# Attention pooling: the fourth group's relu on ScalarE and the softmax steps in one run

## What is computed

```python
h = relu(einsum('bse,eh->bsh', behavior, W_b) + (candidate @ W_c)[:, None, :] + fc1_b)
scores = einsum('bsh,h->bs', h, fc2_w[:, 0]) + fc2_b[0]
attn = softmax(scores, axis=-1)
user_interest = einsum('bse,bs->be', behavior, attn)
z = relu(concatenate([user_interest, candidate], axis=1) @ mlp1_w + mlp1_b)
logit = (z @ mlp2_w + mlp2_b)[:, 0]
```

## Time and profile before

| what | value |
|---|---|
| median of 3 runs | 304.12 us (303.32 to 304.25) |
| the profiled execution's own time | 302.84 us |
| its span, first to last instruction | 301.0 us |
| PE busy | 274.9 us, 91% |
| DVE busy | 255.3 us, 85% |
| ACT busy | 109.7 us, 36% |
| POOL busy | 28.7 us, 10% |
| granted TensorE clock, mean | 0.989 |
| bytes moved by DMA | 105.83 MB |

### The profile page before, as it was taken

The page is one execution under the profiler, slowest core; times in us unless marked ns, Lnnn a source line. Parts: engine busy times, 40 slices in busy tenths (PEclk is TensorE's granted clock), DMA queues, the critical chain, the costliest instruction groups (busy, mean ns, idle before and its releaser), DMA issues.

```text
span 301.0 us, 8104 instructions
## 1 busy us (share of the span) xinstructions
PE 274.9 (91%) x2934; PEld 187.8 (62%) x2934; DVE 255.3 (85%) x437; ACT 109.7 (36%) x267; POOL 28.7 (10%) x38
## 2 busy tenths in 40 slices
PE   6897999999999999999999999999999999999896
PEld 5654676566657666665676656566765666576553
DVE  2699988889988888898888889988888898888661
ACT  4433243443432244334323443442344344323112
POOL 2001001111110011111101111110011111101110
PEclk9599999999999999999999999999999999999999
DMA  7999999999999999999999999999999999750000
GB/s 262 436 425 427 422 427 421 425 427 424 425 432 422 425 432 422 424 407 393 366 376 364 386 376 398 391 354 384 366 367 369 400 396 381 289 216 2 3 0 2
DMA packets 10505, 105.83 MB, mean 352 GB/s; under 512 B 1152, under 2 KB 1664, under 8 KB 2432
## 3 DMA queue, kind: packets, MB, share of 16 engines
q1 hardware_dynamic: 10352, 105.39, 86.3%
q10 hardware_dynamic: 144, 0.31, 0.4%
HBM read 105.70 MB, written 0.00 MB: 351 GB/s over the span
## 4 chain that ended last, share of the span: by engine, by line
PE 67%; issue 13%; DVE 8%; POOL 5%; ACT 3%; DMA 1%; DVEq 1%; ACTq 0%; POOLq 0%
PE u_ps L567 16%; PE z_ps L537 12%; PE z_ps L541 11%; PE z_ps L545 8%; PE z_ps L542 8%; PE s_ps L557 7%; POOL weights_by_row L262 5%; DVE hidden L402 3%; ACT weights L303 2%; DVE xl L392 2%; DMA first_sb<-in_first 1%; PE z_ps L567 1%; DVE exp_bias L430 1%; ACT weights L301 1%; PE u_ps L664 1%
## 5 line engine op out<-in xcount | busy, mean ns | idle before, releaser
L402 DVE TENSOR_TENSOR hidden<-z_ps,neg_bias 128x800 f32<-128x800 f32 x128 | 123.4, 984 | 28.4 <-PE z_ps L545 28.4
L293 ACT CAST xh<-xt 128x800 fp32r<-128x800 f32 x96 | 79.3, 856 | 60.4 <-PE z_ps L545 50.5
L392 DVE TENSOR_TENSOR xl<-xt,xh 128x800 fp32r<-128x800 f32 x96 | 92.4, 963 | 2.0 <-ACT xh L293 1.9
L541 PE MATMUL z_ps<-xh,w_hi 128*128 128x512 f32 x192 | 75.6, 394 | 0.4 <-DVE hidden L402 0.4
L567 PEld LDWEIGHTS u_ps<-x,weights_by_row 128*32 128x32 f32 x1500 | 43.5, 109 | 38.7 <-issue 38.7
L567 PE MATMUL u_ps<-x,weights_by_row 128*32 128x128 f32 x1500 | 50.7, 274 | 17.9 <-POOL weights_by_row L262 11.2
L542 PE MATMUL z_ps<-xh,w_lo 128*128 128x512 f32 x192 | 64.0, 348 | 0.0
L262 POOL TENSOR_TENSOR weights_by_row<-weights,first_sb 128x400 f32<-128x400 f32 x31 | 26.9, 868 | 259.1 <-ACT weights L303 259.1
L545 PE MATMUL z_ps<-xl,w_hi 128*128 128x512 f32 x192 | 51.3, 349 | 0.0
L557 PE MATMUL s_ps<-hidden,f_col 128*1 128x384 f32 (+1 forms) x512 | 49.6, 505 | 1.1 <-DVE hidden L402 1.1
L537 PE MATMUL z_ps<-xt,first_sb 128*128 128x288 f32 (+1 forms) x128 | 48.3, 500 | 0.0
(11 more groups left out here) (69 smaller groups left out, 89.0 us busy)
## 6 DMA issues: line engine op xcount, KB each, us to landing
x<-in_behavior SPq DMA_DIRECT2D x32, 1600.0 KB, 7.7
xt<-in_behavior_t SPq DMA_DIRECT2D x31, 1600.0 KB, 9.3
xt<-in_behavior_t SPq DMA_DIRECT2D x4, 400.0 KB, 5.0
first_sb<-in_first ACTq DMA_DIRECT2D x1, 307.5 KB, 4.3
later_sb<-in_later SPq DMA_DIRECT2D x1, 258.5 KB, 19.2
cand<-in_candidate SPq DMA_DIRECT2D x1, 192.0 KB, 4.8
cand<-in_candidate SPq DMA_DIRECT2D x1, 64.0 KB, 4.2
out_logit<-logit SPq DMA_DIRECT2D x1, 1.8 KB
```

Source lines behind the costliest of these rows:

```text
L293: nc.scalar.copy(xh[g][:, :], xt[q][:, g, :]).then_inc(xh_made, 1)
L392: nc.vector.tensor_tensor(xl[g][:, :], xt[q][:, g, :], xh[g][:, :].bitcast(F32), ALU.subtract).then_inc(xl_made, 1)
L402: nc.vector.tensor_tensor(hidden[q % 2][:, g, :, :].rearrange("p t (b s) -> p t b s", s=PARTS), z, nb.to_broadcast([P, TILES, EACH, PARTS] ...
L541: nc.tensor.matmul(z[:, a:b], w_hi[:, :], xh[g][:, a:b], start=True, stop=False)
```

## The change

ScalarE makes `hidden` for each chunk's fourth group: four activations, one for each of the group's rows, which read that row's columns of the product in PSUM (25 runs of 8 columns), add the row's bias and apply relu. They are counted by a semaphore of their own, `relu_made`; `hidden_made` now counts three maxima a chunk. Since this group holds the true relu and not the value less the bias, the constant `own_row` leaves its rows out of the shift, and ScalarE makes a positive copy of the bias in the period of chunk 0. VectorE drops the fourth maximum and takes the six softmax steps one behind the other, after low half one and before low half two. On ScalarE the exponents move ahead of high half three, and the relus stand behind it. TensorE's waits on banks and on the scores' input go to whichever semaphore counts the group.

```diff
--- before.py
+++ after.py
@@ -115,6 +115,7 @@
         f2_col = sb("f2_col", [P, Q])
         ones = sb("ones", [P, P])
         neg_bias = sb("neg_bias", [P, B])
+        bias = sb("bias", [P, B])
         neg_f2 = sb("neg_f2", [P, 1])
         bias_f2 = sb("bias_f2", [P, B])
         shift_sel = sb("shift_sel", [P, CHUNKS, EACH])
@@ -157,12 +158,14 @@
         setup_step = sem("setup_step")
         neg_f2_made = sem("neg_f2_made")
         bias_f2_made = sem("bias_f2_made")
+        bias_made = sem("bias_made")
         shift_done = sem("shift_done")
         shift_made = sem("shift_made")
         xh_made = sem("xh_made")
         xl_made = sem("xl_made")
         z_done = sem("z_done")
         hidden_made = sem("hidden_made")
+        relu_made = sem("relu_made")
         scores_done = sem("scores_done")
         softmax_step = sem("softmax_step")
         weights_made = sem("weights_made")
@@ -318,6 +321,26 @@
                 act.wait_ge(neg_f2_made, 1)
                 nc.scalar.mul(bias_f2[:, :], neg_bias[:, :], neg_f2[:, :]).then_inc(bias_f2_made, 1)
 
+            def positive_bias(part):
+                a, b = (n * P for n in CAND_PARTS[part])
+                act.wait_ge(setup_step, part + 2)
+                nc.scalar.mul(bias[:, a:b], neg_bias[:, a:b], -1.0).then_inc(bias_made, 1)
+
+            def biased_relu(c, q, phase):
+
+                act.wait_ge(z_done, c * GROUPS + GROUPS)
+                if phase <= 1:
+                    act.wait_ge(bias_made, 1 + phase)
+                if phase >= 2:
+
+                    act.wait_ge(scores_done, c - 1)
+                z = z_view(q, GROUPS - 1)[:, 0:WIDTH].rearrange("p (t r) -> p t r", r=Q)
+                for b in range(EACH):
+                    mine = slice(b * PARTS, (b + 1) * PARTS)
+                    op = nc.scalar.activation(hidden[q % 2][:, GROUPS - 1, :, mine], z[:, :, mine], ACT.Relu,
+                                              bias=bias[:, bass.ds(c * ROWS + (GROUPS - 1) * EACH + b, 1)])
+                op.then_inc(relu_made, 1)
+
             def relu(part, m):
                 a, b = PART_CHUNKS[part]
                 act.wait_ge(z_all_done, 2 * part + m + 1)
@@ -342,12 +365,15 @@
                 next_half(0)
                 next_half(1)
                 if phase == 0:
+                    positive_bias(0)
                     bias_times_f2()
+                    positive_bias(1)
                 if flush:
                     copy_pooled4(c - 2, u_ps)
-                next_half(2)
                 if phase >= 1:
                     exponents(c - 1, (q + 1) % 2, phase <= 2)
+                next_half(2)
+                biased_relu(c, q, phase)
                 if flush:
                     copy_pooled_t(c - 2, u_ps)
 
@@ -465,30 +491,22 @@
             def period(c, q, phase):
                 nq = (q + 1) % X_BUFS
 
-                def step(n):
-                    if phase >= 1:
-                        softmax(c - 1, (q + 1) % 2, n, phase <= 2)
-
                 biased_max(c, q, 0, phase < 2)
                 biased_max(c, q, 1, phase < 2)
                 if phase == 0:
                     negative_bias(1)
                 if phase != LAST:
                     low_half(c + 1, nq, 0)
-                step(0)
+                if phase >= 1:
+                    for n in range(SOFTMAX_STEPS):
+                        softmax(c - 1, (q + 1) % 2, n, phase <= 2)
                 if phase != LAST:
                     low_half(c + 1, nq, 1)
-                step(1)
                 biased_max(c, q, 2, phase < 2)
-                step(2)
                 if phase == 0:
                     shifts()
-                step(3)
-                biased_max(c, q, 3, phase < 2)
-                step(4)
                 if phase != LAST:
                     low_half(c + 1, nq, 2)
-                step(5)
                 if phase == LAST:
                     inverses(0, 0)
 
@@ -522,6 +540,14 @@
 
         @block.tensor
         def _(pe):
+            def banks_read(c, g):
+
+                if g % GROUPS == SPLIT:
+
+                    pe.wait_ge(relu_made, c + (g // GROUPS + 1))
+                else:
+                    pe.wait_ge(hidden_made, c * SPLIT + (g // GROUPS * SPLIT + g % GROUPS + 1))
+
             def products(c, q, g, early):
                 z = z_view(q, g)
                 halves = [(0, BANK), (BANK, WIDTH)]
@@ -530,8 +556,7 @@
                 else:
                     pe.wait_ge(xt_loaded[q], loads(c, q))
                 if not early:
-
-                    pe.wait_ge(hidden_made, c * GROUPS + (g + 1 - Z_BACK[q * GROUPS + g]))
+                    banks_read(c, g - Z_BACK[q * GROUPS + g])
                 if g == SPLIT:
                     for a, b in halves:
                         op = nc.tensor.matmul(z[:, a:b], w_b, xt[q][:, g, a:b], start=True, stop=True)
@@ -548,7 +573,8 @@
             def score(c, buf, early):
                 if early:
                     pe.wait_ge(f2_col_made, 2)
-                pe.wait_ge(hidden_made, c * GROUPS + GROUPS)
+                pe.wait_ge(hidden_made, c * SPLIT + SPLIT)
+                pe.wait_ge(relu_made, c + 1)
                 if not early:
 
                     pe.wait_ge(softmax_step, c * SOFTMAX_STEPS - (SOFTMAX_STEPS - 1))
@@ -582,7 +608,7 @@
                 pe.wait_ge(x_loaded[q], loads(c, q))
                 if q % 2 == 0:
                     pe.wait_ge(masked, c + 1)
-                    pe.wait_ge(hidden_made, CHUNKS * GROUPS)
+                    pe.wait_ge(relu_made, CHUNKS)
                     sum_tiles(c, q, last_pair_ps, 0, TILES).then_inc(pooled_done, 1)
                 else:
                     pe.wait_ge(last_masked, 1)
@@ -622,7 +648,7 @@
                 if part == 0 and m == 0:
                     pe.wait_ge(later_loaded, 16)
 
-                    pe.wait_ge(hidden_made, LAST * GROUPS + 2)
+                    pe.wait_ge(hidden_made, LAST * SPLIT + 2)
                 if part == 1 and m == 0:
                     pe.wait_ge(softmax_step, LAST * SOFTMAX_STEPS + 1)
                 if part == 1 and m == 1:
@@ -716,7 +742,7 @@
     row_mask = p // PARTS == rows
     zeros = np.zeros_like(row_mask)
     each = [p == p.T, np.concatenate([zeros, row_mask, zeros], axis=1), p % Q == np.arange(Q)[None, :],
-            row_mask & (p % PARTS == 0), p % Q // PARTS == np.arange(EACH)[None, :],
+            row_mask & (p % PARTS == 0), (p < SPLIT * Q) & (p % Q // PARTS == np.arange(EACH)[None, :]),
             p // PARTS == p.T // PARTS]
     return [m.astype(np.float32) for m in each]
 
```

## The result

Median 282.93 us (282.43 to 283.49, 4 runs) against 303.72 of the kernel before, a ratio of 0.9317 (95% interval 0.9288 to 0.9345): 20.8 us faster. The prediction had the direction and the mechanism; its 287.4 is 4.5 too high and its range, down to 284.5, misses the time. The profiled execution took 283.16 (span 281.4).

What follows compares the result with a forecast made beforehand. The VectorE order in a loop through GpSimd's mask sets the chunk, 8.67 us against TensorE's 8.03. 28 x 0.64 = 17.9, less 1.0 (start) and 0.25 (end), is 16.7: 304.12 - 16.7 = 287.4 us, range 284.5 to 296.

Steps and rivals of the forecast that it cites:

- 28 chunks: Weighted sums from the chunk behind 37.76 us to the last at 280.87, each to save 0.64: 17.9 us.
- start, transfers: Start of the kernel: a late transfer holds up a high half; loss taken as 1.0 us, between 0 and 3.6.
- end: Last scores wait for the relus instead of the fourth maximum: 0.25 us lost, between 0 and 0.5.
- The loop through the mask: Weighted sum, group three's product, VectorE, exponents, mask, next sum: 8.73 us; opened by the change, mask 3.2 us early.
- The scores take 1.48: TensorE's scores, 1.48 us read at the kernel's end and called seen only there; part of its 7.92 a chunk.
- Worth 0.64 a chunk: Softmax steps in one run on VectorE: opens the loop and removes the mask wait, 0.64 us a chunk.
- The relus: Four on ScalarE, 0.42 each, 1.43 us together (1.0 to 3.4); 0.4 of slack before the scores, cost nothing.
- Rival 1, the shared port: GpSimd's mask holds up VectorE's low half at their shared read port; at the dearest 298 us; chance 0.08.
- Rival 2, the transfers bind: DMA limited to 393 GB/s, so a chunk takes 8.34 us and the kernel 295; chance 0.10.
- the 405 named as a sign of being right: Sign: transfer rate in the second half up to some 405 GB/s.
- Rival 3, the relus set the scores: Relus on ScalarE at 0.86 us each delay the scores, chunk 9.17, 14 us slower, 318; chance 0.05.
- Rival 4, the wait only changes its name: TensorE, freed of the mask, stops for something as late; 0.55 of 0.64 given back, 302 us; chance 0.03.

Runs made afterwards that it cites:

- experiment 1: Kernel before with only the order changed (softmax steps in one run, exponents ahead of high half three), fourth maximum kept on VectorE: 293.93 us, ratio 0.9689.
- experiment 2: Changed kernel with softmax steps spread out again and ScalarE's exponents behind the relus, so only the relus move: 284.11 us, ratio 0.9368.
- experiment 4: Changed kernel with ScalarE's exponents back behind high half three and the relus, run of softmax steps kept: 282.34 us, ratio 0.9308.
- experiment 5: Changed kernel with TensorE's weighted sum ahead of the scores and VectorE's low half two ahead of the softmax steps: 297.8 us, ratio 0.9815.
- experiment 3: Against experiment 2, ScalarE's relus put behind the exponents: 336.9 us, ratio 1.1114 to the kernel before.
- experiment 6: Changed kernel with each relu made twice, first into a spare tile, four more activations a chunk: 308.69 us, ratio 1.0166.
- number 10: Against number 9, second part's candidates' products behind the last weighted sum, last transposes and transposed copy moved earlier: 279.61 us, ratio 0.9204.
- number 8: Changed kernel with the first part's row sums and a candidates' product ahead of the last scores, another behind the last-but-one weighted sum: 281.52 us.
- number 9: Changed kernel with the edits of number 7 and number 8 together: 280.30 us, ratio 0.9209.
- number 11: The changed kernel itself run once more, beside number 9 and number 10 on the same chip: 283.01 us, ratio 0.9305.
- number 7: Changed kernel with every load of x issued one chunk later and the last layers' constants behind x of chunk 3: 280.15 us, ratio 0.9235.

## Why the prediction was right in kind and wrong in size

| step | predicted | measured |
|---|---|---|
| 28 chunks | 28 x 0.64 = 17.9 | 8.67 before, 7.91 after: 28 x 0.765 = 21.4 |
| start, transfers | -1.0 (0 to -3.6) | 37.75 to the next sum 9.62 in place of 7.91: -1.7 |
| end | -0.25 | 301.0 - 280.87 = 20.13, 281.4 - 260.92 = 20.48: -0.35 |
| ahead of them | 0 | +0.2 |
| sum, profiled | 16.7 | 19.6, against 302.84 - 283.16 = 19.7 |

- **The loop through the mask: right.** The wait is gone, the mask 3.2 us early (experiments 1, 2 and 4).
- **The step that failed: "The scores take 1.48".** Its one row has 128x128 weights behind the scores; in a chunk 32-column weights follow, and the term is 1.37. As I read it, the price of going over to full weights stood in the sum twice, in 1.48 and in the 1.62 of the weighted sum: experiment 5 finds the pair at 2.99 to 3.00 in either order, 0.11 under the 3.10 of the sum. 28 x 0.11 = 3.1 us, nearly all of the 3.5 that the chunks lack. The follower and not the end of the kernel makes the 1.48. The trace before has it a second time, in chunk 0, where a product follows (21.03 - 19.55 = 1.48), so "seen only at the end" was wrong too:

```profile
19.55 1.55 PE L557 MATMUL s_ps<-hidden,f_col 128*32 128x416 f32 x16
...
21.03 0.50 PE L541 MATMUL z_ps<-xh,w_hi 128*128 128x512 f32 x1
```

- **The range failed with it.** Its low end allowed for start and end, and nothing for a TensorE sum that rested on one row from another place. The choice of base added to it: the profiled execution before lay 1.3 below the shown median, and the one after 0.2 above its own. With the 19.7 - 16.7 = 3.0 that the sum lacks, these are the 4.5 us. With 1.37 for the scores the forecast would have been 284.3.
- **"Worth 0.64 a chunk" for the run of steps: wrong for the run alone.** Alone it gives 0.31 (8.66 to 8.35), the relus alone 0.67 (to 7.99). I had worked out what VectorE would carry with the run only, 8.2, and not that the old loop less one maximum is 7.83, already below TensorE.
- **The relus: right** in their time, 428 ns, and in their slack, 0.43 against 0.4. An estimate by the Trainium skill, page "ScalarE: Activation LUTs", section "What ACT_TABLE_LOAD costs", is 280 + 0.833 x 200 = 447 ns. The rule in that page's section "Rules for kernel authors" gives relu to VectorE, and experiment 1, which keeps it there, is 11 us slower than the changed kernel (293.93 against 282.93). ScalarE takes 1.38 us for what VectorE does in 0.90, but it had the time.
- **Rival 1, the shared port: no loss here.** Low halves take 987 ns against 963, maxima 988 against 984; VectorE still idles before its maxima. At 162.66 a low half starts 0.14 before the mask is over and takes 1.00. The timetable keeps the two apart; where they meet for longer, the second to start does take longer. In experiment 4 the first mask starts while a low half runs and takes 1.37 in place of 0.87:

```profile
26.73 0.98 DVE L418 TENSOR_TENSOR xl<-xt,xh 128x800 fp32r<-128x800 f32 x1
...
27.06 1.37 POOL L265 TENSOR_TENSOR weights_by_row<-weights,first_sb 128x400 f32<-128x400 f32 x1 [24.71 <-ACT weights L306]
```

  In experiment 5 low halves start some 0.2 before the mask's end, 30 in all, and take 1.05 on average in place of 0.98, this one 1.09:

```profile
170.74 0.87 POOL L265 TENSOR_TENSOR weights_by_row<-weights,first_sb 128x400 f32<-128x400 f32 x1 [7.66 <-ACT weights L306]
...
171.37 1.09 DVE L418 TENSOR_TENSOR xl<-xt,xh 128x800 fp32r<-128x800 f32 x1 [0.63 <-ACT xh L296]
```

- **Rival 2, the transfers bind: only at the start.** They move 422 to 433 GB/s in the second half, so 393 was not their rate, and the 405 named as a sign of being right was too low as well. **Rival 3, the relus set the scores:** not as built, but experiments 3 and 6 show both ways there. **Rival 4, the wait only changes its name:** no, chunks are 7.91.

## What to carry over

When a wait is found between two engines, write down the whole loop that passes through it and take each piece of work off it in turn: here one instruction less in the loop was worth twice as much as the new order, and, with the old order on VectorE, the same relus one place later in ScalarE's queue made the kernel 11% slower than before the change. A duration from start to start holds only for the same follower, so a term that is seen once, in another place, needs bounds of its own in the range. And once the loop's wait is gone, look at the start: the transfers' order there was worth another 2.8 us.

## What the runs showed of the hardware

- How long a run of matmuls with 32-column weights lasts, start to start, depends on what follows it. The 100 of the weighted sum last 1.35 us when the scores follow (experiment 5) and 1.62 when 128x128 weights follow. The 16 of the scores last 1.37 us when the weighted sum follows, 1.48 before 128x128 weights at the start and the end of the kernel, and 1.65 before them behind a weighted sum (experiment 5).
- From the end of ScalarE's last relu to the start of the scores that wait for it pass 0.24 us (experiment 6) and 0.28 (experiment 3).
- A low half on VectorE, with both inputs in SBUF, and GpSimd's mask hold each other up: a mask of 0.87 us took 1.37 (experiment 4, once) and low halves of 0.98 took 1.05 on average and up to 1.11 (experiment 5), each as the second to start.
- Where the granted clock falls near the start differs between executions. Its mean is 0.60 in 8 to 16 us before and after the change and 0.58 in number 10, 0.79 in 16 to 24 us in numbers 8, 9 and 11, 0.79 in 24 to 32 us in number 1, and 1.00 in all of these in the other traces. In numbers 2 to 5 that record is not the whole: the 512-column pass shown above takes 0.63 us there between 12.4 and 14.9 us, as in number 10's slow stretch, at a clock given as 1.00. First scores start at 19.61 without a fall (number 7), at 19.89 with an early one (number 10) and at 21.38 with one in 16 to 24 us (number 9).
